# A decoder layer in float32: feed-forward weights and context loaded already transposed

## The reference, cut to what matters

```python
x = x + attn(layernorm(x))                 # 32 heads of 16, one shared k/v head, ALiBi, causal
x = x + xattn(layernorm(x), ctx, ctx, ...) # 32 heads of 128, 8 k/v heads, rotary, k and v from ctx
xf = layernorm(x)
up   = einsum('td,fd->tf', xf, W_up)       # W_up, W_gate: 1376 x 512
gate = silu(einsum('td,fd->tf', xf, W_gate))
x = x + einsum('tf,df->td', gate * up, W_down)   # W_down: 512 x 1376
```

## Time and profile before

| | us |
|---|---|
| three runs | 1031.92, 1030.58, 1029.69 |
| median | 1030.58 |
| the profiled execution: span | 1029.7 |
| self-attention, to the barrier | about 236 |
| cross-attention, to the barrier | about 236 to 828 |
| feed-forward: opening and tiles, output rows | about 828 to 966, 966 to 1027 |

### The profile page before, as it was taken

The page is one execution under the profiler, slowest core; times in us unless marked ns, Lnnn a source line. Parts: engine busy times, 40 slices in busy tenths (PEclk is TensorE's granted clock), DMA queues, the critical chain, the costliest instruction groups (busy, mean ns, idle before and its releaser), DMA issues. The chain is left out here.

```text
span 1029.7 us, 16071 instructions
## 1 busy us (share of the span) xinstructions
PE 1003.1 (97%) x5260; PEld 822.9 (80%) x5260; DVE 581.3 (56%) x973; ACT 428.1 (42%) x1239; POOL 381.6 (37%) x375
## 2 busy tenths in 40 slices
PE   5999999989999999999999999999999999999998
PEld 3787777876888888888888888888887778888787
DVE  3765555636776666767666666766765852222101
ACT  2777666751533433533533434434334433332100
POOL 7422222253642642643634534626424222222100
PEclk8999999989999999999999999999999999999999
DMA  6000000211110210210210201201100022221001
GB/s 199 12 11 11 11 10 10 62 52 52 50 54 1 73 32 0 71 31 0 74 27 20 72 10 31 61 10 49 43 1 32 1 62 61 61 69 47 11 31 41
DMA packets 45699, 39.98 MB, mean 39 GB/s; under 512 B 3617, under 2 KB 34465, under 8 KB 45665
## 3 DMA queue, kind: packets, MB, share of 16 engines
q1 hardware_dynamic: 45280, 38.48, 12.7%
q0 software_dynamic: 384, 1.05, 0.3%
HBM read 37.43 MB, written 2.10 MB: 38 GB/s over the span
## 5 line engine op out<-in xcount | busy, mean ns | idle before, releaser
L624 PE MATMUL bank<-cross_wo_hl,cross_outT_hl 128*128 128x512 f32 x768 | 191.7, 398 | 1.0 <-POOL cross_wo_hl L618 0.6
L624 PE MATMUL bank<-hsT_hl,cross_wqkv_hl 128*128 128x512 f32 x768 | 188.2, 394 | 0.0
L624 PEld LDWEIGHTS bank<-cross_wo_hl,cross_outT_hl 128*128 128x128 f32 x768 | 143.1, 188 | 35.5 <-POOL cross_wo_hl L618 1.6
L624 PEld LDWEIGHTS bank<-hsT_hl,cross_wqkv_hl 128*128 128x128 f32 x768 | 141.9, 188 | 29.3
L938 ACT ACTIVATE cross_scores<-cross_scores,cross_negmax 128x128 f32<-128x128 f32 x256 | 99.8, 391 | 127.1 <-DVE cross_negmax L876 127.1
L798 POOL TENSOR_TENSOR cross_qT<-rotated,rotated_other_half 128x512 f32<-128x512 f32 x64 | 82.8, 1293 | 162.0 <-DVE rotated_other_half L840 162.0
L624 PE MATMUL bank<-hsT_hl,ff_gate_upT_hl 128*128 128x512 f32 (+1 forms) x528 | 126.3, 395 | 0.5 <-DVE ff_gate_upT_hl L1140 0.5
L624 PEld LDWEIGHTS bank<-hsT_hl,ff_gate_upT_hl 128*128 128x128 f32 (+1 forms) x528 | 96.3, 186 | 21.9 <-DVE ff_gate_upT_hl L1140 0.8
L948 ACT CAST cross_outT_hl<-bank 128x512 fp32r<-128x512 f32 x64 | 37.1, 579 | 143.4 <-PE bank L624 142.5
L838 DVE TENSOR_TENSOR rotated<-bank,cosT 128x512 f32<-128x512 f32 x80 | 55.2, 690 | 71.4 <-PE bank L624 71.2
L624 PE MATMUL bank<-ctxT_hl,cross_wqkv_hl 128*128 128x512 f32 x384 | 94.3, 394 | 1.1 <-PEq L74 1.1
(11 more groups left out here) (121 smaller groups left out, 1565.7 us busy)
## 6 DMA issues: line engine op xcount, KB each, us to landing
staged_rows<-in_wq SPq DMA_DIRECT2D x32, 256.0 KB, 2.8
staged_rows<-in_wo SPq DMA_DIRECT2D x32, 256.0 KB, 2.7
staged_rows<-in_wg SPq DMA_DIRECT2D x10, 256.0 KB, 2.6
staged_rows<-in_wu SPq DMA_DIRECT2D x10, 256.0 KB, 2.8
staged_rows<-in_wd SPq DMA_DIRECT2D x10, 256.0 KB, 3.0
ctx_tok<-in_ctx SPq DMA_DIRECT2D x8, 256.0 KB, 2.6
staged_rows<-in_wk SPq DMA_DIRECT2D x8, 256.0 KB, 3.1
staged_rows<-in_wv SPq DMA_DIRECT2D x8, 256.0 KB, 3.1
```

What stands on the lines that cost most here:

```text
L624: i = nc.tensor.matmul(out, stationary[:, a], moving[:, b], start=(first and k == 0), stop=(last and k == 2))
```

## The change

The host lays out four inputs differently: `wg`, `wu` and `wd` are given transposed, and each sequence of the context is given with its 512 columns on the partitions, as [128, 4 x 128]. The kernel loads them into the same staging slots and `ctx_tok`. All their transposes on TensorE are left out, and with them the semaphores `ctx_transposed`, `w_transposed` and `wd_transposed`. ScalarE's casts wait for the loads themselves and read SBUF; VectorE's subtractions read the same SBUF rows; the loads of the next tile, or of the next sequence, wait for VectorE's subtraction. TensorE no longer waits for `ctx_low`.

```diff
             with sp.Fori(1, SEQS) as b:
-                sp.wait_ge(sem["ctx_transposed"], b)
+                sp.wait_ge(sem["ctx_low"], b)
                 load_ctx(b)
...
-                        nc.vector.tensor_tensor(block_of(ctxT[:, 1], b), G[1][:].rearrange("p (t k) -> p t k", t=KT),
+                        nc.vector.tensor_tensor(block_of(ctxT[:, 1], b), ctx_tok[:].rearrange("p (t k) -> p t k", t=KT),
...
-                        act.wait_ge(sem["ctx_transposed"], b + 1)
-                        nc.scalar.copy(block_of(ctxT[:, 0], b), G[1][:].rearrange("p (t k) -> p t k", t=KT)).then_inc(sem["ctx_high"], 1)
+                        act.wait_ge(sem["ctx_loaded"], 16 * b + 16)
+                        nc.scalar.copy(block_of(ctxT[:, 0], b), ctx_tok[:].rearrange("p (t k) -> p t k", t=KT)).then_inc(sem["ctx_high"], 1)
...
                     if s == 7 and not since(b, 1):
-                        pe.wait_ge(sem["ctx_low"], b + 1)
                         q_transposes(b + 1, 0)
...
-                    if s == 5 and scores:
-                        pe.wait_ge(sem["ctx_loaded"], 16 * b + 16)
-                        if front:
-                            pe.wait_ge(sem["q_copied"], b + 2)
-                        transpose4(G[1], ctx_tok, "ctx_transposed")
...
                     if s == 7 and front and since(b, 1):
-                        pe.wait_ge(sem["ctx_low"], b + 1)
                         q_transposes(b + 1, 0)
...
     for k, name in enumerate(("wg", "wu")):
-        if not (isinstance(i, int) and i == 0):
-            sp.wait_ge(sem["w_transposed"], 2 * i + k - 1)
-            if k == 1:
-                sp.wait_ge(sem["wd_transposed"], i)
-        sp.dma_start(m["gate_up_rows"][0:n, k, :], io[name][bass.ds(at, n), :]).then_inc(sem[f"{name}_loaded"], 16)
-    sp.dma_start(m["down_rows"][:, :, 0:n], io["wd"].rearrange("(t p) f -> p t f", p=P)[:, :, bass.ds(at, n)]).then_inc(sem["wd_loaded"], 16)
+        if later:
+            sp.wait_ge(sem["w_low"], 2 * i + k - 1)
+        sp.dma_start(m["gate_up_cols"][:, k, :, 0:n], io[name].rearrange("(t p) f -> p t f", p=P)[:, :, bass.ds(at, n)]).then_inc(sem[f"{name}_loaded"], 16)
+    if later:
+        sp.wait_ge(sem["wd_low"], i)
+    sp.dma_start(m["down_rows"][0:n, :], io["wd"][bass.ds(at, n), :]).then_inc(sem["wd_loaded"], 16)
...
-                nc.vector.tensor_tensor(wT[:, k, 1, :, 0:n], TW[k][:].rearrange("p (t f) -> p t f", t=KT)[:, :, 0:n],
+                nc.vector.tensor_tensor(wT[:, k, 1, :, 0:n], raw[:, k, :, 0:n],
...
-                nc.vector.tensor_tensor(wdT[0:n, 1, bass.ds(i, 1), :], TD[0:n, :].unsqueeze(1), wdT[0:n, 0, bass.ds(i, 1), :].bitcast(F32),
+                nc.vector.tensor_tensor(wdT[0:n, 1, bass.ds(i, 1), :], rawd[0:n, :].unsqueeze(1), wdT[0:n, 0, bass.ds(i, 1), :].bitcast(F32),
...
-                act.wait_ge(sem["w_transposed"], 2 * i + k + 1)
+                act.wait_ge(sem["wg_loaded" if k == 0 else "wu_loaded"], 16 * i + 16)
                 if not first:
                     act.wait_ge(sem["ff_product"], products_by(i - 1, k, 1))
-                nc.scalar.copy(wT[:, k, 0, :, 0:n], TW[k][:].rearrange("p (t f) -> p t f", t=KT)[:, :, 0:n]).then_inc(sem["w_high"], 1)
+                nc.scalar.copy(wT[:, k, 0, :, 0:n], raw[:, k, :, 0:n]).then_inc(sem["w_high"], 1)
...
-                act.wait_ge(sem["wd_transposed"], i + 1)
-                nc.scalar.copy(wdT[0:n, 0, bass.ds(i, 1), :], TD[0:n, :].unsqueeze(1)).then_inc(sem["wd_high"], 1)
+                act.wait_ge(sem["wd_loaded"], 16 * i + 16)
+                nc.scalar.copy(wdT[0:n, 0, bass.ds(i, 1), :], rawd[0:n, :].unsqueeze(1)).then_inc(sem["wd_high"], 1)
...
-            def w_transposes(i, k, first=False):
...
-                w_transposes(i, 1, first)
-                pe.wait_ge(sem["wd_loaded"], 16 * i + 16)
-                if not first:
-                    pe.wait_ge(sem["wd_low"], i)
-                for t in range(KT):
-                    e = nc.tensor.transpose(TD[0:n, t * P:(t + 1) * P], rawd[:, t, 0:n], ident[:])
-                e.then_inc(sem["wd_transposed"], 1)
...
                     product(i, 0, first, halves=(1,))
-                    w_transposes(i + 1, 0)
                     product(i, 1, first, halves=(1,))
                     return
                 product(i, 0)
-                if not (isinstance(i, int) and i == FT - 1):
-                    w_transposes(i + 1, 0)
                 product(i, 1)
...
+    given["ctx"] = _np.ascontiguousarray(given["ctx"].transpose(0, 2, 1).reshape(SEQS, KT, P, P).transpose(0, 2, 1, 3).reshape(SEQS, P, DM))
+    for name in ("wg", "wu", "wd"):
+        given[name] = _np.ascontiguousarray(given[name].T)
```

More of the change, by code:

```diff
@@ L689, in load_ff_rows @@
     at = i * P if isinstance(i, int) else sp.snap(i * P)
+    later = not (isinstance(i, int) and i == 0)
     for k, name in enumerate(("wg", "wu")):
-        if not (isinstance(i, int) and i == 0):
-            sp.wait_ge(sem["w_transposed"], 2 * i + k - 1)
-            if k == 1:
-                sp.wait_ge(sem["wd_transposed"], i)
-        sp.dma_start(m["gate_up_rows"][0:n, k, :], io[name][bass.ds(at, n), :]).then_inc(sem[f"{name}_loaded"], 16)
-    sp.dma_start(m["down_rows"][:, :, 0:n], io["wd"].rearrange("(t p) f -> p t f", p=P)[:, :, bass.ds(at, n)]).then_inc(sem["wd_loaded"], 16)
+        if later:
[4 more added lines that the diff above has]
+    sp.dma_start(m["down_rows"][0:n, :], io["wd"][bass.ds(at, n), :]).then_inc(sem["wd_loaded"], 16)
 def half_of(t, half):
@@ L1082, in feed_forward @@
 def feed_forward(nc, m, sem, ps, io):
-    GATE, UP, TW, TD, YB = ps[0:2], ps[2:4], ps[4:6], ps[6], [ps[7], ps[6]]
-    x, hsT, ident, raw, rawd = m["x"], m["hsT_hl"], m["ident"], m["gate_up_rows"], m["down_rows"]
+    GATE, UP, YB = ps[0:2], ps[2:4], [ps[7], ps[6]]
+    x, hsT, raw, rawd = m["x"], m["hsT_hl"], m["gate_up_cols"], m["down_rows"]
     LATE = {7: GATE[1], 8: UP[1], 9: YB[0]}
@@ L1212, in _ @@
         def _(pe):
-            def w_transposes(i, k, first=False):
-                n = width_of(i)
-                pe.wait_ge(sem["wg_loaded" if k == 0 else "wu_loaded"], 16 * i + 16)
-                if not first:
-                    pe.wait_ge(sem["w_low"], 2 * i + k - 1)
-                for t in range(KT):
-                    e = nc.tensor.transpose(TW[k][:, t * P:t * P + n], raw[0:n, k, t * P:(t + 1) * P], ident[0:n, 0:n])
-                e.then_inc(sem["w_transposed"], 1)
             def product(i, k, first=False, halves=(0, 1)):
@@ L1253, in body @@
                 product(i, 0)
-                if not (isinstance(i, int) and i == FT - 1):
-                    w_transposes(i + 1, 0)
                 product(i, 1)
-            w_transposes(0, 0, first=True)
             body(0, first=True)
@@ L1278 @@
 SEMAPHORES = """x_first rel_loaded head_of_row_loaded wkv1_loaded wq1_loaded x_rest pos_loaded wo1_loaded mask_loaded
-ctx_loaded ctx_transposed ident_zero ident_ready exponent_ready ones_ready mv0 mv1 var_eps0 var_eps1 rstd0 rstd1
+ctx_loaded ident_zero ident_ready exponent_ready ones_ready mv0 mv1 var_eps0 var_eps1 rstd0 rstd1
 kv_high kv_copied scores1 kexp bias tables_loaded stats0 stats1 xn_transposed xn_centred hs_centred xn wk8 mask_is_set exp1 biased1 max1 ctx_high
@@ L1285 @@
 norm_stats norm_mv norm_var_eps norm_rstd norm_rows norm_transposed norm_high norm_low wg_loaded wu_loaded wd_loaded
-w_transposed w_high w_low wd_transposed wd_high wd_low ff_product silu h_product h_high h_low y3 x3""".split() + [f"piece_loaded{slot}" for slot in range(SLOTS)]
+w_high w_low wd_high wd_low ff_product silu h_product h_high h_low y3 x3""".split() + [f"piece_loaded{slot}" for slot in range(SLOTS)]
 def program(nc, io):
@@ L1298, in program @@
             "stage": stage,
-            "gate_up_rows": stage[:, 0:2, :],
-            "down_rows": stage[:, 2, :].rearrange("p (t f) -> p t f", t=KT),
+            "gate_up_cols": stage[:, 0:2, :].rearrange("p k (t f) -> p k t f", t=KT),
+            "down_rows": stage[:, 2, :],
             "norm_rows": stage[:, 3:5, :],
```

## The result

Over four executions the changed kernel takes 1013.46 us in the median (1012.19 to 1017.90), beside 1030.47 for the kernel before: a ratio of 0.984, 95% interval 0.982 to 0.987. The prediction was 1014.3, faster, with a range of 1011.5 to 1018.0.

The account below looks back on a forecast made before the run. TensorE's queue was taken to bound the feed-forward tiles and the middle self-attention sequences. Terms 12.9 + 0.3 + 3.1 = 16.3 us, so 1030.58 - 16.3 = 1014.3 us, range 1011.5 to 1018.0.

Parts of the forecast that it names:

- Feed-forward transposes: Feed-forward loop: 28 groups of four transposes at 0.44 us and two at 0.33 leave TensorE's queue, 12.9 us.
- The cross-check: Feed-forward loop: 114.5 us less 18.5 products of 5.49 us (101.6) leave 12.9 us for the transposes.
- Opening: Feed-forward stage start: VectorE's subtraction no longer waits for ScalarE's cast, 0.3 us; bounds 0 and 1.06.
- Context transposes: Self-attention: sequences 1 to 6 give 2.6 us, sequence 0 gives 0.5, sequence 7 nothing; sum 3.1 us.
- the wait of 1.84: TensorE's wait at 220.62, end of self-attention: sequence 7's removed group only lengthens it by 0.44 us, worth 0.
- Costs taken as nothing: ScalarE's casts, VectorE's subtractions, later-freed staging slots, load waits and TensorE's opening gap were each costed at 0.
- The cover: Feed-forward tiles: cast and subtraction finish 1.84 us (gate) or 2.68 (up) after weights are freed; next user 5.49 behind.
- more than 2 us ahead: Sign of being right: feed-forward subtractions still done more than 2 us ahead of their product.
- (b): Self-attention: the gain is lost at POOL, contending with VectorE's two-SBUF-input subtraction; all 3.1 us lost gives 1017.4; chance 0.08.
- (a): Feed-forward opening: TensorE's clock falls in the gap, costing 2.9 to 4.5 us, 1017.2 to 1018.8; chance 0.15.
- (c): Feed-forward tiles: weights late, TensorE waits where it transposed, all 12.9 us come back, 1027.2; chance 0.04.
- (d): Feed-forward tiles: staging slot held until the subtraction becomes the bound; at 13.0 us landings 1047, slower; chance 0.03.

Follow-up runs that it names:

- The two halves: Feed-forward weights changed alone, context still transposed on TensorE: 1016.30 us; context changed alone, feed-forward weights still transposed on TensorE: 1027.35 us.
- The two kernels with the transposes put back: Changed kernel plus 30 groups of four transposes nobody reads, at their old places: 1026.66 us; a tile's groups in one place: 1026.25 us.
- the memset: Changed kernel with POOL's subtraction cut to 8 of every 512 columns, the rest zeroed once by POOL and left out of the products: 1019.15 us.
- the context half: Context part of the change alone, feed-forward weights still transposed on TensorE: 1027.35 us, ratio 0.997 to the kernel before.
- the doubled cover: Changed kernel with ScalarE's cast and VectorE's subtraction of the loop's gate and up tiles done twice: 1012.93 us.

## Why the prediction was right

**What bounds the kernel** held: the chain named TensorE's queue, and taking from the queue took from the time. The two halves, run singly, gave 14.5 and 3.5 us; the steps had 13.2 and 3.1.

**Feed-forward transposes, 12.9: mis-sized by 1.0.** Tiles and output rows together went from 191.08 to 177.19, 13.89 less. The term counted pieces of the chain at 0.44; each block of transposes also costs 0.05 at its edges, and about twenty blocks went. The cross-check could not find this, since it used the 5.49 us of a product that stands between transposes: both workings came from the same rows and carry the same error. The two kernels with the transposes put back, at 12.30 and 12.25 us a tile, show the edge cost itself.

**Opening, 0.3: 0.41.** From VectorE's statistics at the stage's start to the first unbroken product it was 835.47 - 828.67 = 6.80 and is 831.42 - 825.03 = 6.39. VectorE's wait of 0.30 went, as said, and a tenth more.

**Context transposes, 3.1: 3.3.** Six sequences brought 3.56 - 0.88 = 2.68 (2.6 said), sequence 0 brought 0.59 (0.5 said, of bounds 0.30 and 0.74). Cross-attention starts 3.63 earlier, of which 0.29 belong to the start of the kernel. That the group of sequence 7 is worth 0 was right: POOL's chain, and with it TensorE's wait, moved by what sequences 0 to 6 gave, 3.57 and 3.55. Wrong in the detail: the wait of 1.84 did not become 0.4 longer; the time appeared earlier, as a wait of 0.34 for ScalarE's probabilities at 207.41.

The sum: 13.89 + 0.41 + 3.34 + 0.29 = 17.9 us between the two profiled executions, against 16.3 said. The medians differ by 17.0, so the forecast was 0.8 us too long. Part of the difference between 17.9 and 17.0 is in the choice of the base: the prediction took the profiled execution for the shortest of three because its span is as long as the shortest time. With the 1.8 us outside the span that every run here shows, 1029.7 belongs to an execution of some 1031.5, one of the longer ones. So it is in part luck that the forecast came within 0.8 us: its three terms were 1.3 us too small (16.3 against 17.6), and the difference of the medians came out smaller than that of the two profiled executions.

**Costs taken as nothing.** The casts from SBUF took 614 ns (628 said). VectorE's subtraction keeps its 0.69 alone (0.66 to 0.69), but beside POOL it takes 1.50, above the upper bound of 1.23: that bound was another engine's price for the work and not the price of a conflict. It cost nothing all the same. The cover, named at more than 2 us, is 3.6 us for the gate weights but just under 2 for the up weights: they are ready 3.48 us after their product frees them instead of 2.68, and the difference is the longer subtraction. The sign "more than 2 us ahead" so failed by a little for the up weights; the cover still stood twice the work. The Trainium skill, "GPSIMD Engine Reference", section "Specifications", which the prediction set beside rival (b), has the contention, and the trace agrees with it. The Trainium skill, "SBUF — State Buffer", section "SBUF: two separate sides", has it more closely: POOL shares a pair of ports with a VectorE instruction that has two SBUF inputs, if POOL's reads SBUF too, or that runs in a two-port mode, and whichever starts first holds the pair for its whole instruction while the other is blocked. The trace agrees: the subtraction that starts 0.34 us behind POOL's ends 0.55 behind it. The normalisation that ends 0.3 us behind the memset reads one SBUF tensor, and would be the second case; which mode it ran in no run shows.

**Rivals.** (a): in the changed kernel's profiled execution the clock stayed at 1.00 in the opening, through a gap of 2.67 us, and filling the gap changed no median. The Trainium skill, "TensorE: Matmul & The Clock Gate", section "Why this matters for your kernels", warns of long idle gaps between matmul bursts, behind which the clock is back at half rate; the trace agrees behind the gap of 4.62 us, where it fell to 0.50. At the end of self-attention it fell behind a wait of only 1.84 us with short matmuls around it. (b) fell with the context half, (c) with the doubled cover. (d) did not come up, with landings of 2.8 and 2.9 us; a late landing was not tried.

## What to carry to other kernels

Where the chain that ended last is one engine's queue without waits, an instruction taken out is worth its length and the change-over around it: take the pace of the unbroken work from a stretch that has none of the removed instructions, not from the pieces between them. A step moved off that queue is free as long as its cover is: put twice the work there and see. And a short wait among small matmuls can cost more by the clock behind it than by itself; products that nobody reads, put into such waits, are cheap to try. The host's own transposing is not in the time measured here.

## What the runs showed that was not expected

- VectorE's fp32 subtraction of two SBUF tensors, 128x512: 0.69 us alone, 1.50 when it meets POOL's subtraction, which keeps its 1.29. With its source in PSUM it kept 0.69 beside POOL. A normalisation of 0.54 us from SBUF to SBUF took 4.83 behind a memset of POOL.
- A block of transposes among fp32 products costs 0.05 us beside its own length: 24 matmuls take 5.49 us instead of 5.44.
- 17 added products of 512 columns made the profiled execution 2.7 us shorter: the clock stayed at 2.4 GHz where it had been at 1.2 for 10 us.
- Some executions, 4 of 31, are 4 to 5 us longer, and no cause was found.
